# A four-layer graph kernel on one core: TensorE's passes written out, one addition moved to VectorE, and a new interleaving of two groups

## The chip, the cores and the metric

The kernel runs on one core of one Trainium2 chip. The metric is the time of one execution in microseconds, measured on the device; lower is better. The kernel before takes 2250.71 us (median of 3 runs, 2248.42 to 2252.54).

## The reference, cut to what matters

128 boards of 64 tokens with 256 features each go through four layers. Each layer adds its output to x:

```python
h = relu(layernorm(x)); x = x + att0(h, adj)    # layer 0: 8 heads of 32, biases, six fixed masks and two from adj
h = relu(layernorm(x)); x = x + att1(h, adj)    # layer 1: 4 heads of 64, all masked by adj
h = relu(layernorm(x)); x = x + graph(h, adj)   # layer 2
h = relu(layernorm(x)); x = x + att3(h, adj)    # layer 3: as layer 1

def graph(h, adj):                              # 4 heads
    Wh = h @ W[head].T + bW[head];  e = Wh @ attn[head]
    A = tanh(where(adj, e @ Wh.T, 0))
    hp = relu(A @ Wh)
    ha = concat(hp) @ A_w.T;  hf = h @ fc_w.T
    c = sigmoid(hf @ g1_w.T + ha @ g2_w.T + gbias)
    return hf * c + ha * (1 - c)
```

The kernel computes the last line with the update of x as x + ha + 0.5 * (hf - ha) * (1 + tanh(z / 2)), where z is the argument of the sigmoid. So ha itself is added to x once: this is the addition that the change moves.

## The kernel before, in words

Four boards (256 tokens) are a group; there are 32 groups. Two groups are in work at a time, one in each of two slots, and each slot has its own buffers and four of the eight PSUM banks. A pass takes one group through each slot, so there are 16 passes.

A group's work is a list of 109 steps (lines 287 to 304), the same for all engines: `bn`, `stats`, `norm` (the layer norm), `turn` 0 and 1 (transposes of the normalised x), `q`, `k`, `v`, `scores`, `mask`, `max`, `soft`, `pt` (transposes of the probabilities), `heads`, `pv`, `out` for an attention layer; `r`, `e` 0 to 3, `h`, `s2`, `a`, `ah`, `hp`, `ha`, `hf`, `hat` (transposes of ha), `g`, `sum` for the graph layer. Every engine walks through this list and issues only what is its own in a step. Engines wait for each other through semaphores, whose values are counted from the pass number (`Counts`, line 124).

Matrices are split in two parts of reduced width, high and low, and multiplied in three products. ScalarE copies the high part of a result out of PSUM, VectorE then computes the low part, and TensorE needs both for what follows.

The order in which an engine takes the steps of the two slots is written out per engine in `ORDER` (line 100): a lag, and for each of slot 0's 109 steps the number of slot 1's steps that follow it. Slot 1 is behind by the lag; so in the first half of a pass slot 0 goes through layers 0 and 1 while slot 1 does its graph layer and layer 3 of the group before, and in the second half the roles are changed. `passes` (line 306) writes out the first pass, without slot 1's older steps. The 15 others are one loop of each engine (`eng.Fori`, line 326) over a body that is written once; at its head the values for the waits are worked out in registers (`eng.snap`). The rest of slot 1's last group follows the loop. TensorE's last step in the body is slot 1's `r`, VectorE's is slot 1's `e` 0, ScalarE's is slot 0's last `pv`.

GpSimd (line 393) has three kinds of work: the power -0.5 for each layer norm in `stats` (line 410), between VectorE's variance (line 941) and VectorE's normalisation (line 949); the row terms in `r` (line 415), which TensorE's `s2` reads (line 650); and in `hat` the addition of ha to x (line 423), which VectorE's `sum` waits for (line 1093). x of the next group of a slot is loaded by SyncE (line 350) as soon as the last `out` of the group before has been added (line 1028), and stored from another buffer.

Of the kernel before, what the change touches and what calls it, by code (L numbers as in the profile page):

```python
# [25 lines left out]
ALU = mybir.AluOpType  # L26
# [36 lines left out]
def constants():  # L63
# [22 lines left out]
    for part in (0, LO):  # L86
# [11 lines left out]


ORDER = {  # L100
# [5 lines left out]
    "act": (57, (  # L106
# [4 lines left out]
    "dve": (48, (  # L111
# [4 lines left out]
    "pool": (46, (  # L116
# [4 lines left out]
}  # L121


# [16 lines left out]
def build(nc, x_in, adjq_in, adjt_in, mats_in, cols_in, rows_in, cst_in, out):  # L140
    GROUPS = x_in.shape[0] // TOK
    ITERS = GROUPS // SLOTS
# [6 lines left out]
    with ctx:  # L149
# [23 lines left out]
        X, XN, HT, MASKA, MASKO, ADJ8, ADJT8, SMALL = ([] for _ in range(8))  # L173
# [45 lines left out]
        WIDE, AT, F, RS, CT = ([] for _ in range(5))  # L219
# [83 lines left out]
                       ("g", L2, 0), ("g", L2, 1), ("sum", L2, 0)])  # L303
        STEPS = att_steps(0) + att_steps(1) + L2_STEPS + att_steps(2)

        def passes(eng, step, order):

            n = len(STEPS)  # L310
            lag, merge = order
            assert len(merge) == n and sum(merge) == n

            def turn(first, now, before):
                done = 0
                for k in range(n):
                    step(0, STEPS[k], now)
                    for done in range(done + 1, done + merge[k] + 1):
                        if done > lag:
                            step(1, STEPS[done - lag - 1], now)  # L320
                        elif not first:
                            step(1, STEPS[n - lag + done - 1], before)

            turn(True, Counts(0), None)
            if ITERS > 1:
                with eng.Fori(0, ITERS - 1) as i:
                    turn(False, Counts(i + 1, eng.snap), Counts(i, eng.snap))
            last = Counts(ITERS - 1)
            for k in range(n - lag, n):
                step(1, STEPS[k], last)  # L330
# [62 lines left out]
        @block.gpsimd  # L393
        def _(pool):
            nc.gpsimd.memset(RAWR[SQ:P, :], 0.0).then_inc(setup["padded"], 1)
            pool.wait_ge(setup["padded"], 1)
            nc.gpsimd.memset(UPAD[:, :, :], 0.0)
            nc.gpsimd.memset(BPAD[:, :, :], 0.0)
            for s in range(SLOTS):
                last = nc.gpsimd.memset(ADJT8[s][:, :, :, :], 0.0)  # L400
            last.then_inc(setup["zeroed"], 1)

            def step(s, what, v):
                k, a, i = what
                sm = S[s]
                if k == "stats":

                    n = norm_count(a, v)
                    pool.wait_ge(sm["ve"], n)
                    nc.gpsimd.tensor_tensor(RSTD[s], VE[s], HALF.broadcast_to([P, TT]), ALU.pow  # L410
                                            ).then_inc(sm["rstd"], 1)
                elif k == "r":

                    pool.wait_ge(sm["r_lo"], v.once)
                    nc.gpsimd.tensor_tensor(
                        R4[s][:, :].rearrange("p (b h q) -> p b h q", h=H2, q=SQ),
                        RS[s][:, 0:TOK].bitcast(F32).rearrange("p (b q) -> p b q", q=SQ).unsqueeze(2).broadcast_to([P, NB, H2, SQ]),
                        HEADS.unsqueeze(1).unsqueeze(3).broadcast_to([P, NB, H2, SQ]), ALU.mult
                        ).then_inc(sm["r4_ready"], 1)
                elif k == "hat" and i == 0:  # L420

                    pool.wait_ge(sm["ha_sb"], v.once)
                    nc.gpsimd.tensor_tensor(X[s][:, :], X[s][:, :], F[s][:, 0:512], ALU.add).then_inc(sm["x_ha"], 1)  # L423

            pool.wait_ge(setup["consts"], 1)

            pool.wait_ge(setup["vec_ps"], 2)
            for s in range(SLOTS):
                last = nc.gpsimd.memset(RS[s][:, 0:TOK].bitcast(F32), 0.0)
            last.then_inc(setup["terms_zero"], 1)  # L430
            passes(pool, step, ORDER["pool"])


        @block.tensor
        def _(pe):
# [289 lines left out]
                else:  # L725
                    att(s, k, a, i, v)

            passes(pe, step, ORDER["pe"])


        @block.scalar
# [134 lines left out]
        def _(dve):  # L866
# [164 lines left out]
            def l2(s, k, i, v):  # L1031
                sm, n = S[s], v.once
# [22 lines left out]
                elif k == "s2":  # L1055

                    if i == 0:
                        dve.wait_ge(sm["adjT_in"], v.dma2)
                    dve.wait_ge(sm["tanh"], v.two[i])
                    seen = ADJT8[s][:, i, :, :].unsqueeze(2).broadcast_to([P, 2, H2, SQ])  # L1060
                    view = tanh_buf(s, i).rearrange("p (e h q) -> p e h q", e=2, h=H2)
                    tt(view, view, seen, ALU.mult).then_inc(sm["at_f"], 1)  # L1062
                elif k == "a":
                    dve.wait_ge(sm["at_hi"], v.two[i])
                    lo_part(AT[s][:, 1, i, :], tanh_buf(s, i), AT[s][:, 0, i, :]).then_inc(sm["at_lo"], 1)

                    dve.wait_ge(sm["rs_hi"], v.two[i])
                    at = slice(i * 512, i * 512 + 512)
                    lo_part(RS[s][32:SQ, at], bank(s, i)[32:SQ, :], RS[s][32:SQ, at]).then_inc(sm["rs_lo"], 1)
                elif k == "ah":  # L1070
                    at = slice(i * 512, i * 512 + 512)
                    for c in range(DC):
                        dve.wait_ge(sm["ah_hi"], v.four[2 * i + c])
                        lo_part(WIDE[s][:, 1, c, at], bank(s, 2 * (1 - i) + c), WIDE[s][:, 0, c, at]
                                ).then_inc(sm["ah_lo"], 1)
                elif k == "hp":
                    dve.wait_ge(sm["ct_hi"], v.four[i])
                    hi, lo = ((CT[s][:, 0, :], CT[s][:, 1, :]) if i % 2 == 0 else (AT[s][:, 0, 0, :], AT[s][:, 1, 0, :]))
                    stt(lo, bank(s, HEAD_BANKS[i % 2]), 0.0, hi.bitcast(F32), ALU.max, ALU.subtract).then_inc(sm["ct_lo"], 1)
                elif k == "hat":  # L1080
                    dve.wait_ge(sm["hat_hi"], v.two[i])
                    at = slice(i * TOK, i * TOK + TOK)
                    lo_part(CT[s][:, 1, at], bank(s, HAT_BANKS[i])[:, 0:TOK], CT[s][:, 0, at]).then_inc(sm["hat_lo"], 1)
                elif k == "g":

                    dve.wait_ge(sm["gate_t"], v.two[i])
                    diff = F[s][:, 512 + i * D:512 + i * D + D]
                    tt(diff, bank(s, G_BANKS[i])[:, 0:D], F[s][:, i * D:i * D + D], ALU.subtract).then_inc(sm["diff"], 1)
                    dve.wait_ge(sm["diff"], v.two[i])
                    stt(diff, XN[s][:, i * D:i * D + D], 1.0, diff, ALU.add, ALU.mult).then_inc(sm["gated"], 1)  # L1090
                elif k == "sum":

                    dve.wait_ge(sm["x_ha"], n)
                    dve.wait_ge(sm["gated"], v.two[1])
                    stt(X[s][:, :], F[s][:, 512:1024], 0.5, X[s][:, :], ALU.mult, ALU.add).then_inc(sm["res2"], 1)
# [44 lines left out]
```

## Time and profile before

| | before |
|---|---|
| median of 3 runs | 2250.71 us (2248.42 to 2252.54) |
| the profiled execution | 2248.06 us |
| its span, first to last instruction | 2245.9 us |
| TensorE busy | 2011.9 us, 90% of the span |
| VectorE busy | 1445.6 us, 64% |
| ScalarE busy | 1151.8 us, 51% |
| GpSimd busy | 192.2 us, 9% |
| mean granted TensorE clock | 0.967 of full speed |
| bytes moved by DMA | 30.66 MB |

The page gives the busy time of each engine, the span in 40 slices, the chain of work that ended last, and groups of instructions. Busy shares are means over the whole span. What TensorE waits for, and where in a pass, is read from the table of waits and from the timeline. In the timeline a row is an instruction or a few of one kind: start, duration, engine, line, operation, what it writes and reads, how many, and in brackets the time that the engine stood idle before it and what ended that. PE is TensorE, PEld its weight loads, DVE VectorE, ACT ScalarE, POOL GpSimd, SP SyncE.

### The profile page before, as it was taken

What the parts mean: (1) busy time and instruction counts of PE and PEld (TensorE: products, weight loads), DVE (VectorE), ACT (ScalarE), POOL (GpSimd) and SP (SyncE); (2) the same over time, 40 slices, a digit from 0 to 9 for tenths busy, and PEclk for the clock granted to TensorE, in tenths of its full rate; (3) what the DMA queues carried; (4) which work ended last, traced back from release to release, by engine and by line L of the source; (5) the groups of instructions that cost most, each with busy time, mean ns of one, the idle gap of its engine ahead of it and who ended that gap; (6) DMA issues with size and microseconds to landing.
All of it is one profiled execution on the core that took longest, in us unless ns stands there. A gap on an engine that the chain in (4) does not pass through costs nothing.

```text
span 2245.9 us, 53566 instructions
## 1 busy us (share of the span) xinstructions
PE 2011.9 (90%) x21228; PEld 1818.6 (81%) x21228; DVE 1445.6 (64%) x3769; ACT 1151.8 (51%) x3862; POOL 192.2 (9%) x203
## 2 busy tenths in 40 slices
PE   6699989899898989989899998989989899998997
PEld 5588878788887888878788887888888788887885
DVE  4466667667666667667666666666757666666663
ACT  3355555455455555555455454545455455455552
POOL 0000101100001100100110000100101100000100
PEclk8799999999999999999999999999999999999998
DMA  5000000000000000000000000000000000000000
GB/s 174 1 3 12 12 12 12 11 5 9 12 12 12 11 11 2 11 12 11 12 11 2 12 11 12 11 11 2 11 12 11 11 12 2 12 11 12 11 6 5
DMA packets 40630, 30.66 MB, mean 14 GB/s; under 512 B 15664, under 2 KB 40240, under 8 KB 40432
## 3 DMA queue, kind: packets, MB, share of 16 engines
q1 hardware_dynamic: 40432, 27.48, 4.1%
q8 instruction: 190, 3.11, 0.6%
q14 instruction: 8, 0.07, 0.0%
HBM read 19.08 MB, written 8.39 MB: 12 GB/s over the span
## 4 chain that ended last, share of the span: by engine, by line
PE 62%; issue 18%; DVE 12%; ACT 4%; POOL 4%; DMA 1%; DVEq 0%; SPq 0%; POOLq 0%; ACTq 0%
PE ps L437 57%; PE ps L505 4%; POOL small L410 3%; DVE small L931 2%; DVE xn L949 2%; PE ps L581 2%; ACT probs L788 1%; DVE x L1028 1%; DVE wide L1053 1%; DVE f L1062 1%; POOL x L423 1%; DVE aT L870 1%; ACT f L824 1%; ACT wide L816 1%; DVE small L938 1%
## 5 line engine op out<-in xcount | busy, mean ns | idle before, releaser
L437 PE MATMUL ps<-hT,w_hi 128*128 128x256 f32 x2560 | 511.2, 291 | 55.8 <-issue 47.7
L437 PEld LDWEIGHTS ps<-hT,w_hi 128*128 128x128 f32 x2560 | 420.5, 194 | 73.1 <-issue 50.8
L788 ACT ACTIVATE probs<-probs,small 128x64 f32<-128x64 f32 x1024 | 342.1, 339 | 33.2 <-DVE small L1009 31.4
L437 PE MATMUL ps<-hT,w_lo 128*128 128x256 f32 x1280 | 343.1, 288 | 0.0
L437 PEld LDWEIGHTS ps<-hT,w_lo 128*128 128x128 f32 x1280 | 249.2, 195 | 2.7
L437 PE MATMUL ps<-w_hi,hT 128*128 128x256 f32 (+1 forms) x1024 | 249.1, 312 | 0.0
L410 POOL TENSOR_TENSOR small<-small,consts 128x2 f32<-128x2 f32 x128 | 88.8, 694 | 1776.2 <-DVE small L941 1776.2
L437 PE MATMUL ps<-w_hi,oT 128*128 128x256 f32 x768 | 189.2, 311 | 27.4 <-DVE oT L870 27.4
L437 PE MATMUL ps<-wide,w_hi 128*128 128x256 f32 x1024 | 213.1, 285 | 0.2
L788 ACT ACTIVATION_READ_ACCUMULATOR probs<-probs,small 128x1 f32 x1024 | 196.2, 192 | 0.0
L816 ACT ACTIVATE wide<-ps,c_vec 128x256 fp32r<-128x256 f32 x256 | 107.6, 472 | 148.3 <-PE ps L437 148.3
L437 PEld LDWEIGHTS ps<-w_hi,hT 128*128 128x128 f32 x1024 | 175.4, 188 | 8.4
L1053 DVE SCALAR_TENSOR_TENSOR wide<-ps,c_vec,wide 128x256 fp32r<-128x256 f32 x256 | 109.5, 479 | 103.6 <-ACT wide L816 103.5
L437 PEld LDWEIGHTS ps<-w_hi,oT 128*128 128x128 f32 x768 | 147.5, 211 | 32.5 <-DVE oT L870 32.3
L437 PEld LDWEIGHTS ps<-wide,w_hi 128*128 128x128 f32 x1024 | 163.4, 188 | 3.1 <-DVE wide L870 0.7
L949 DVE TENSOR_SCALAR xn<-x,small 128x256 f32<-128x256 f32 x256 | 123.3, 523 | 62.0 <-POOL small L410 59.7
L437 PE MATMUL ps<-w_hi,cT 128*128 128x256 f32 x768 | 159.3, 290 | 0.3 <-ACT cT L848 0.3
L505 PE MATMUL ps<-consts,xn 128*128 128x128 f32 x512 | 116.3, 324 | 46.1 <-DVE xn L949 42.9
L437 PE MATMUL ps<-w_lo,hT 128*128 128x256 f32 (+1 forms) x512 | 149.9, 310 | 0.0
L763 ACT ACTIVATE hT<-ps 128x256 fp32r<-128x256 f32 x256 | 88.4, 383 | 98.5 <-PE ps L505 97.6
L505 PEld LDWEIGHTS ps<-consts,xn 128*128 128x128 f32 x512 | 62.5, 151 | 86.9 <-DVE xn L949 74.2
L437 PE MATMUL ps<-wide,w_lo 128*128 128x256 f32 x512 | 131.8, 280 | 0.0
(123 smaller groups left out, 4342.5 us busy)
## 6 DMA issues: line engine op xcount, KB each, us to landing
raw_mats<-mats SPq DMA_DIRECT2D x8, 1024.0 KB, 11.9
x<-x SPq DMA_DIRECT2D x32, 256.0 KB, 3.0
out<-xn SPq DMA_DIRECT2D x32, 256.0 KB, 3.0
adj<-adjq SPq DMA_DIRECT2D x64, 16.0 KB, 2.0
adjT<-adjt SPq DMA_DIRECT2D x64, 8.0 KB, 2.1
raw_consts<-board_consts SPq DMA_DIRECT2D x1, 451.5 KB, 3.1
raw_rows<-rows SPq DMA_DIRECT2D x1, 256.0 KB, 4.5
bias_cols<-cols SPq DMA_DIRECT2D x1, 6.0 KB, 3.6
```

Source lines behind the costliest of these rows:

```text
L410: nc.gpsimd.tensor_tensor(RSTD[s], VE[s], HALF.broadcast_to([P, TT]), ALU.pow).then_inc(sm["rstd"], 1)
L423: nc.gpsimd.tensor_tensor(X[s][:, :], X[s][:, :], F[s][:, 0:512], ALU.add).then_inc(sm["x_ha"], 1)
L437: return nc.tensor.matmul(o, lhsT, rhs, start=start, stop=stop, skip_group_check=True)
L505: last = nc.tensor.transpose(bank(s, H_BANKS[c])[:, t * P:t * P + P], XN[s][:, t * D + c * P:t * D + c * P + P], IDENT)
L581: last = nc.tensor.transpose(bank(s, 1 - i)[:, at:at + P], PR[s][:, j, at:at + P], IDENT)
L763: fn(HT[s][:, 0, c, :], bank(s, H_BANKS[c])[:, 0:TOK], ACT.Relu).then_inc(S[s]["hT_hi"], 1)
L788: last = fn(p, p, ACT.Exp, bias=ROWMAX[s][:, row:row + 1], accum_out=ROWSUM[s][:, row:row + 1])
L816: last = fn(e_view(s, 0, oc, i), e_bank(s, E_BANKS[i], oc), ACT.Identity, bias=CVEC[:, oc, i:i + 1])
L824: fn(tanh_buf(s, i), bank(s, 2 + i), ACT.Tanh).then_inc(sm["tanh"], 1)
L931: nc.vector.bn_stats(STATS[s][:, t, :], X[s][:, t * D:t * D + D]).then_inc(S[s]["bn"], 1)
L949: ts(XN[s][:, t * D:t * D + D], X[s][:, t * D:t * D + D], MV[s][:, t, 0:1], RSTD[s][:, t:t + 1], ALU.subtract, ALU.mult).then_inc(S[s]["xn ...
L1053: stt(e_view(s, 1, oc, i), e_bank(s, E_BANKS[i], oc), CVEC[:, oc, i:i + 1], e_view(s, 0, oc, i).bitcast(F32), ALU.add, ALU.subtract).then_ ...
```

## The change

Three things are changed.

1. TensorE's passes are written out one behind the other, with constants in place of registers in the waits. The other engines keep their loops.
2. The addition of ha to x is taken from GpSimd's step `hat` and put into VectorE's step `hat` 0, ahead of VectorE's low parts there. It has the same wait (`ha_sb`, set by ScalarE's copy of ha at line 844) and raises the same semaphore.
3. The lags and merge lists of all four engines are replaced. TensorE's lag goes from 49 to 48, ScalarE's from 57 to 46, VectorE's stays at 48, GpSimd's goes from 46 to 37.

```diff
 ORDER = {
-    "pe": (49, (
+    "pe": (48, (
...
-    "act": (57, (
+    "act": (46, (
...
     "dve": (48, (
...
-    "pool": (46, (
+    "pool": (37, (
...
-        def passes(eng, step, order):
+        def passes(eng, step, order, unrolled=False):
...
             turn(True, Counts(0), None)
-            if ITERS > 1:
+            if unrolled:
+                for i in range(1, ITERS):
+                    turn(False, Counts(i), Counts(i - 1))
+            elif ITERS > 1:
                 with eng.Fori(0, ITERS - 1) as i:
                     turn(False, Counts(i + 1, eng.snap), Counts(i, eng.snap))
...
-                elif k == "hat" and i == 0:
-
-                    pool.wait_ge(sm["ha_sb"], v.once)
-                    nc.gpsimd.tensor_tensor(X[s][:, :], X[s][:, :], F[s][:, 0:512], ALU.add).then_inc(sm["x_ha"], 1)
...
-            passes(pe, step, ORDER["pe"])
+            passes(pe, step, ORDER["pe"], unrolled=True)
...
                 elif k == "hat":
+                    if i == 0:
+
+                        dve.wait_ge(sm["ha_sb"], n)
+                        tt(X[s][:, :], X[s][:, :], F[s][:, 0:512], ALU.add).then_inc(sm["x_ha"], 1)
                     dve.wait_ge(sm["hat_hi"], v.two[i])
```

The merge lists, written as sequences (0: and 1: are the slots; layers are 0, 1, graph, 3), differ in these places:

```
TensorE, end of slot 1's layer 3:  before  1:heads, 0:turn 0 1, 1:out 0 1, 0:r          after  1:heads, 1:out 0, 0:turn 0 1, 1:out 1, 0:r
TensorE, slot 1's graph layer:     before  1:ha 1, 0:pt 0, 1:hp 3, 0:pt 1, 1:hf 0       after  1:ha 1, 1:hp 3, 0:pt 0, 0:pt 1, 1:hf 0
TensorE, last of the body:         before  1:r                                          after  1:r, 1:e 0
VectorE, end of slot 1's layer 3:  before  1:soft, 0:out 0 1, 0:bn 0, 1:soft, 0:bn 1, 0:stats, 0:norm, 1:pv 0 1, 0:turn 0, 1:out 0, 0:turn 1, 1:out 1
                                   after   0:out 0, 1:soft, 1:soft, 0:out 1, 0:bn 0 1, 0:stats, 1:pv 0 1, 0:norm, 1:out 0, 0:turn 0 1, 1:out 1
VectorE, start of a group:         before  e 3, h, masks, (s2 0), turn 0, turn 1        after  e 3, masks, turn 0, h, turn 1, s2 0
ScalarE, start of slot 0's group:  before  1:e 3, 1:h, 1:s2 0, 0:turn 0 1, 1:s2 1       after  1:e 3, 0:turn 0, 1:h, 0:turn 1, 1:s2 0 1
ScalarE, last of the body:         before  0:pv 1 of layer 3                            after  1:e 2
GpSimd, slot 0's graph layer:      before  0:stats, 0:r, 1:stats of layer 0             after  0:stats, 1:stats of layer 0, 0:r
```

In the last row the power of slot 1's next group stands ahead of the row terms of slot 0.

## Rows read from the trace of the kernel before

**Rows 1.** The page: span, and each engine's busy time, share, instructions.
```profile
span 2245.9 us, 53566 instructions
...
PE 2011.9 (90%) x21228; PEld 1818.6 (81%) x21228; DVE 1445.6 (64%) x3769; ACT 1151.8 (51%) x3862; POOL 192.2 (9%) x203
```

**Rows 2.** PE's waits, whole run: total us, times, longest us.
```profile
PE ps L437 <- issue: 50.0, 18, 3.8
...
PE ps L505 <- DVE xn L949: 42.9, 59, 4.9
```

**Rows 3.** Stretches with the jump: length, busy time (instructions), PE's clock, DMA share.
```profile
408.63:477.60 68.97, 61.52 (x660) 55.59 (x659) 44.29 (x117) 35.48 (x120) 5.92 (x7) 0.98 0.04 10
...
sum 973.08, PE 868.62 PEld 786.73 DVE 620.86 ACT 497.08 POOL 82.96; mean PE 62.04 PEld 56.20 DVE 44.35 ACT 35.51 POOL 5.93
```

**Rows 4.** The same of the 13 stretches without it.
```profile
342.91:408.63 65.72, 61.47 (x660) 55.79 (x659) 44.63 (x117) 35.28 (x120) 5.93 (x8) 0.97 0.04 10
477.60:541.94 64.34, 60.07 (x660) 54.38 (x659) 44.63 (x117) 35.17 (x120) 5.93 (x7) 1.00 0.04 10
...
sum 843.34, PE 787.85 PEld 713.95 DVE 580.38 ACT 457.83 POOL 77.09; mean PE 60.60 PEld 54.92 DVE 44.64 ACT 35.22 POOL 5.93
```

**Rows 5.** Timeline of PE at the jump: last of "r", first of "e".
```profile
1912.77 0.86 PE L437 MATMUL ps<-hT,u_vec 128*36 128x256 f32 x6
...
1916.90 0.36 PE L437 MATMUL ps<-hT,w_hi 128*128 128x256 f32 x1 [3.27 <-issue]
```

**Rows 6.** Timelines of ACT and DVE at the same jump.
```profile
1918.61 0.84 ACT L816 ACTIVATE wide<-ps,c_vec 128x256 fp32r<-128x256 f32 x2 [4.47 <-PE ps L437]
...
1919.48 0.88 DVE L1053 SCALAR_TENSOR_TENSOR wide<-ps,c_vec,wide 128x256 fp32r<-128x256 f32 x2 [4.83 <-ACT wide L816]
1920.27 0.74 DVE L931 BATCH_NORM_STATS2 small<-x 128x6 f32<-128x256 f32 x2
```

**Rows 7.** Timeline of PE where the first pass enters the loop.
```profile
168.79 0.86 PE L437 MATMUL ps<-hT,u_vec 128*36 128x256 f32 x6
169.49 0.36 PE L437 MATMUL ps<-hT,w_hi 128*128 128x256 f32 x1
```

**Rows 8.** DMA queue of instructions, 1886.82 to 1955.62 (jump), then 1955.62 to 2019.97: packets, MB.
```profile
q8 instruction: 7, 0.11, 0.7%
...
q8 instruction: 5, 0.08, 0.5%
```

**Rows 9.** Timelines of POOL, DVE and PE around the addition of ha.
```profile
2019.97 1.28 POOL L423 TENSOR_TENSOR x<-x,f 128x512 f32<-128x512 f32 x1
...
2020.05 1.68 DVE L949 TENSOR_SCALAR xn<-x,small 128x256 f32<-128x256 f32 x2 [0.81 <-POOL small L410]
...
2025.28 0.69 DVE L1095 SCALAR_TENSOR_TENSOR x<-f,x 128x512 f32<-128x512 f32 x1
...
2027.27 0.68 DVE L989 COPY kT<-ps 128x512 f32<-128x512 f32 x1
2028.18 0.73 DVE L949 TENSOR_SCALAR xn<-x,small 128x256 f32<-128x256 f32 x2 [0.23 <-POOL small L410]
...
2021.46 0.87 PE L505 MATMUL ps<-consts,xn 128*128 128x128 f32 x4 [0.55 <-DVE xn L949]
...
2028.06 0.69 PE L437 MATMUL ps<-kT,qT 64*64 64x64 f32 x32
```

**Rows 10.** Timelines of SP, POOL and PE at slot 0's "s2"; the page's landing of x.
```profile
1981.57 0.38 SPq L350 DMA_DIRECT2D x<-x  x1
...
1982.64 1.92 POOL L415 TENSOR_TENSOR row_terms<-rs,consts 128x1024 fp32r<-128x1024 f32 x1 [4.89 <-DVE rs L1048]
1986.10 0.69 POOL L410 TENSOR_TENSOR small<-small,consts 128x2 f32<-128x2 f32 x1 [1.55 <-DVE small L941]
...
1989.71 0.39 PE L437 MATMUL ps<-row_terms,sel_rows 128*128 128x512 f32 x1
...
x<-x SPq DMA_DIRECT2D x32, 256.0 KB, 3.0
```

32 rows, old and new, of the table ORDER are left out of this document.

## The prediction

> **What bounds the kernel now.** I read the page first: TensorE (PE) is busy 90% of the span, VectorE 64%, ScalarE 51%, GpSimd 9% [rows 1]. So the end is set by PE and by what it waits for. The table of PE's waits comes next [rows 2]: the largest single entry is "issue", 50.0 us in 18 pieces, time in which PE waited for no engine; behind it come waits for VectorE's normalised x. To see where these fall I cut the steady part into halves of a pass, from one GpSimd addition of the graph layer's output (line 423) to the next; the addition is made once for each of the 32 groups of four boards. Between 272.48 and 2088.90 us they alternate: 14 halves hold the jump from the end of PE's loop body (slot 1's step "r") back to its start, 13 do not. PE does the same 660 matmuls in each, but the 14 sum to 973.08 us, 69.51 each [rows 3], and the 13 to 843.34 us, 64.87 each [rows 4]. Those 13 are of two kinds: eight of 64.3 to 64.4 us at full granted clock, five of 65.6 to 65.8 with the clock at 0.97 [rows 4].
>
> The jump itself: after the six small matmuls of "r" PE stands still for 3.27 us with nothing to wait for [rows 5]; the 14 pieces in the other passes are 3.2 to 3.8 us. ScalarE and VectorE then wait 4.47 and 4.83 us, all of it PE's lateness [rows 6]. Is it the jump, or the register arithmetic at the head of the body that works out the values of the waits? The first pass is written out and falls into the loop body through that same head without a jump: there "e" follows "r" at once, 0.70 us after its start, with no gap [rows 7]. So it is the jump. What it does is seen in the instruction queue's DMA: 7 blocks of 16 KB in a half with the jump, 5 in one without [rows 8].
>
> **Part 1: PE's passes written out.** Removed: 14 jumps (15 looped passes; the entry and the exit cost none). What follows at a place without a jump is shown by the straight halves, which do the same work, so I use them as the price: 973.08 - 14 x 64.87 = 64.9 us. The gaps themselves are at most 50.0 of them [rows 2]; the rest is that TensorE is at the lower of its clocks, 1.2 instead of 2.4 GHz, for a few us more in such halves (PE busy is 62.04 us in them against 60.60) [rows 3, 4]. I take the mean of the straight halves and not the fastest (64.34), since short waits remain that let the clock fall in some halves: that is the choice in this term. With no fall at all the saving would be 973.08 + 843.34 - 27 x 64.34 = 79.2 us; with a fall in every half (65.72 [rows 4]) it would be 973.08 + 843.34 - 27 x 65.72 = 42.0 us. Added: nothing on PE but a longer stream. 5 blocks per 64.3 us were fetched in straight halves without any gap, so I price streaming at 0.
>
> The Trainium skill, "Runtime: NRT & Kernel Launch", section "Instruction fetch mechanics", says that an engine prefetches instructions only in sequence, 16 KiB at a time, that PE holds 2048 of them and the other engines 512, and that a jump outside this window waits for a fetch. The trace agrees for PE, which runs about 2,650 instructions a pass (21228 matmuls and as many weight loads over 16 passes [rows 1]) and fetches two blocks more when it jumps. By the rule ScalarE (3862 / 16 = 241 instructions a pass) and VectorE (3769 / 16 = 236 [rows 1]) need no fetch at their own jumps, which stay; were it otherwise, rival 2 below would be the forecast.
>
> **Part 2: the addition moves from GpSimd to VectorE.** Before: GpSimd adds for 1.28 us at 2019.97; VectorE's two normalisations (line 949), which start 0.08 us later, take 1.68 us, against 0.73 for the same pair where GpSimd is quiet, and PE waits 0.55 us for them before its transposes [rows 9]. After: that pair costs 0.73, so 0.95 less on VectorE; the addition there costs one 128x512 operation, for which I take the 0.69 us of the similar line 1095 [rows 9]. VectorE's chain behind it is thus 0.26 us earlier. PE's transposes could start 0.55 us earlier, but four steps on PE's "scores" start at 2028.06 while VectorE's copy of k, which they need, ends at 2027.95 [rows 9]: only 0.11 us of slack, so PE keeps 0.25, not 0.55. 32 groups x 0.25 = 8.0 us gained. Bounds: a gain of 0.55 x 32 = 17.6; or, if the slow pair were not GpSimd's doing, VectorE is 0.69 later, of which two idle moments of about 0.17 each before its next operations absorb half: a loss of 0.35 x 32 = 11 us. I take 8.0, nearest to the row of the quiet pair.
>
> On this the Trainium skill, "SBUF — State Buffer", section "SBUF: two separate sides", says that VectorE and GpSimd share one pair of ports, held by one of them for a whole instruction. By that the 0.95 us return in full (the gain of 8.0); by a reading in which the norms are slow for another reason the loss of 11 stands. The trace sides with the rule, 1.68 against 0.73.
>
> **Part 3: the turns laid out anew.** From the merge lists: on PE, in the halves where slot 1 ends its last attention layer, "out" 0 of slot 1 goes ahead of slot 0's graph-layer transposes, where before it followed them; "hp" 3 moves ahead of "pt" 0 there; the jump's place moves by one "e". The wait before those transposes was 0.46 us for VectorE's x; now PE waits about as long for VectorE's low part of the heads' output instead. VectorE does "pv" (0.75) while GpSimd's power runs (0.8 us in which it was idle), but its layer sum comes one 0.42 us operation later. I price this at 0, bounds -0.46 and +0.46 us in each of 16 halves: -7 to +7 us. On ScalarE and VectorE the second transposed half is taken before the first tanh or masking, and masked scores ahead of a remainder; each swaps neighbours of 0.4 to 0.7 us whose readers are later steps: 0, within the same bounds. ScalarE's and VectorE's jumps stay, and GpSimd's; old waits of 4.47 and 4.83 us lay over them [rows 6], VectorE's first operation behind its jump (bn) began as the one before it ended. No row shows these jumps uncovered; bounds 0 and, from that cover, 4.8 us each time; I take 0 because their entries into the loop and their instruction fetches show nothing [rows 7, 8].
>
> GpSimd: slot 1's first power now stands ahead of slot 0's row terms (line 415). Before, these ran 1982.64 to 1984.56 and the power at 1986.10; now they queue behind the power: 1986.79 + 1.92 = 1988.71. PE reads them at 1989.71 [rows 10]. Slack 1.0 us: cost 0, but this cover is thin, and the power waits for x from HBM, issued at 1981.57 and landing in 3.0 us [rows 10].
>
> **Sum.** Against the profiled execution, 2248.06 us (span 2245.9 [rows 1] and 2.2 around it): 2248.06 - 64.9 - 8.0 + 0 = 2175.2 us. The median before is 2250.71, 2.65 more; the same offset gives 2177.8. I say 2177.
>
> **Rivals.**
> 1. *TensorE's clock falls in every half.* The waits of 0.5 to 1.1 us around "pt" and "heads" stay and nothing anchors them to the jump. For: all 14 halves with the jump show less than full clock, and five straight ones do. Against: eight straight halves run at 1.00 [rows 4]. Time: 2248.06 - 42.0 - 8.0 = 2198, on the median's scale 2201.
> 2. *The other engines' jumps come to light.* They sit at the same place (VectorE's behind slot 1's "e" 0, ScalarE's now between "e" 2 and "e" 3, with "s2" waiting for all four), and so far a wait of 4.5 us lay over them. For: there was always cover, so nothing excludes it. Against: rows 7 and 8 as above. If they cost 3.27 us like PE's: 14 x 3.27 = 46 back, 2178 + 46 = 2224.
> 3. *Slower than before: row terms behind x.* The chain x from HBM, bn, power, row terms, "s2" has 1.0 us of slack. If slot 1's x lands late, slot 0's "s2" stands with it, on PE, in 16 halves. To eat the 73 us gained it must be 1.0 + 73/16 = 5.6 us late each time, a landing of 8.6 us instead of 3.0; at 10 us it is 16 x 6.0 = 96 lost, 2274. Against: the median landing is 3.0 us [rows 10], and the DMA engines are busy 4% of a half [rows 4].
> 4. *The change does not do what it says:* the written-out stream stalls at block borders as it did at the jump. 5 blocks a half without a gap [rows 8] speak against; one 3.27 us stall a half would leave no gain (2250).
>
> **Chances.** Forecast with its own spread (2152 to 2192: the saving of part 1 up to 79, parts 2 and 3 by their bounds) 0.68; rival 1 0.18; rival 2, in whole or part, 0.08; rival 3 0.03; rival 4 0.03. The low end is 2248.06 - 79.2 - 17.6 = 2151, plus the offset 2154; I go to 2153. The high end takes in rival 1 and a little of rival 2: 2206. A measurement of this kernel tells 0.2% (4.5 us) from nothing: faster 0.94, within 0.03, slower 0.03.
>
> **What would show it.** Right: PE's "issue" waits fall from 50 to a few us; the gap between "r" and "e" is gone in every pass; all halves are alike, near 64.6 us (64.87 - 0.25); the pair at line 949 beside the addition takes 0.73; the wait of 0.55 before the transposes is gone; instruction blocks fall by two a pass. Wrong: granted clock below 1.00 in each half (rival 1); VectorE or ScalarE idle between its "e" steps once a pass with PE waiting at "s2" (rival 2); PE waiting for row terms (rival 3); an addition that costs VectorE more than 0.69.

## The result: 2.7% faster, at the slow end of the forecast

| | median | ratio to before, 95% interval |
|---|---|---|
| before | 2251.62 us (4 runs) | |
| changed | 2193.66 us (4 runs, 2188.86 to 2197.49) | 0.9734 [0.9697, 0.9771] |
| changed again, in another series | 2188.44 us (before there: 2262.61) | 0.9672 [0.9649, 0.9694] |

The forecast was 2177 (2153 to 2206). The sign, the range and the leading cause hold; 17 us are missing on that scale, 13.7 in the profiled execution (2188.86 against 2175.2).

The medians of the kernel before differ between series (2251.6, 2266.5, 2262.6, 2256.8, 2254.4), so ratios are taken within a series.

The page after, span and engines, answers to [rows 1]; then the page's instruction queue, which before had 190 packets:

```profile
span 2186.7 us, 52980 instructions
PE 1994.9 (91%) x21228; PEld 1808.3 (83%) x21228; DVE 1464.7 (67%) x3801; ACT 1150.5 (53%) x3862; POOL 151.3 (7%) x171
...
q8 instruction: 167, 2.74, 0.5%
```

PE's waits after, as [rows 2] (in the changed kernel most lines are one less than before: 504 is the transposes of x, 948 the normalisation, 436 the products):

```profile
PE ps L580 <- DVE probs L1018: 48.1, 54, 3.3
PE ps L504 <- DVE xn L948: 42.1, 21, 4.9
PE ps L436 <- DVE oT L869: 38.8, 49, 0.9
PE ps L436 <- issue: 18.4, 36, 0.7
```

"Issue" has fallen from 50.0 us to 18.4 and no piece is over 0.7. Most of what is left are pieces of 0.52 us ahead of "heads", at a place where the kernel before waited 0.56 us for ScalarE's copy; the gap of the jump is gone. But the wait for VectorE's normalised x is as large as before, 42.1 against 42.9, and in 21 pieces instead of 59: something new waits there.

The halves, from one addition of ha to the next as in [rows 3, 4]. The first two rows are a neighbouring pair at full clock, the third one in which the clock fell, the last the sum of 28 halves:

```profile
533.06:596.77 63.71, 60.13 (x660) 54.62 (x659) 44.23 (x119) 35.09 (x120) 4.67 (x5) 1.00 0.04 10
596.77:661.91 65.14, 60.07 (x660) 54.51 (x659) 45.72 (x120) 35.39 (x120) 4.63 (x5) 1.00 0.04 10
...
466.48:533.06 66.58, 61.53 (x660) 55.95 (x659) 45.93 (x120) 35.52 (x120) 4.63 (x5) 0.97 0.04 10
...
sum 1821.72, PE 1698.67 PEld 1544.13 DVE 1261.71 ACT 988.52 POOL 130.24; mean PE 60.67 PEld 55.15 DVE 45.06 ACT 35.30 POOL 4.65
```

28 halves take 65.06 us each on the mean; 64.62 was forecast. The half that had the jump went from 68.8 to 63.7. The half that had none went from 64.34 [rows 4] to 65.14, although PE's busy time in it is the same (60.07): it has got slower by 0.8, and its VectorE is busy 1.1 us longer (45.72 against 44.63).

**Where that is.** Timelines of POOL, DVE and PE of the changed kernel at slot 0's "e" steps in such a half; the last DVE row is the same place 64 us earlier, in the good half:

```profile
625.81 0.69 POOL L413 TENSOR_TENSOR small<-small,consts 128x2 f32<-128x2 f32 x1 [7.69 <-DVE small L940]
626.47 1.91 POOL L418 TENSOR_TENSOR row_terms<-rs,consts 128x1024 fp32r<-128x1024 f32 x1
...
624.39 0.74 DVE L930 BATCH_NORM_STATS2 small<-x 128x6 f32<-128x256 f32 x2
...
626.62 2.23 DVE L948 TENSOR_SCALAR xn<-x,small 128x256 f32<-128x256 f32 x2
...
628.58 0.87 PE L504 MATMUL ps<-consts,xn 128*128 128x128 f32 x4 [1.56 <-DVE xn L948]
...
562.91 0.73 DVE L948 TENSOR_SCALAR xn<-x,small 128x256 f32<-128x256 f32 x2
```

GpSimd's row terms now start 0.15 us ahead of the two normalisations, and these take 2.23 us instead of 0.73: they end at 628.85, 0.47 us after the row terms (628.38). In [rows 9] the pair also ends 0.48 us after GpSimd's addition. PE waits 1.56 us. It is the case of [rows 9] once more, with the row terms in the addition's part. x itself was there in time: bn (line 930) starts as VectorE's step before it ends.

At the old place, the addition moved as forecast. DVE and PE of the changed kernel there:

```profile
596.12 0.73 DVE L948 TENSOR_SCALAR xn<-x,small 128x256 f32<-128x256 f32 x2 [0.80 <-POOL small L413]
596.77 0.68 DVE L1083 TENSOR_TENSOR x<-x,f 128x512 f32<-128x512 f32 x1
...
602.91 0.69 DVE L988 COPY kT<-ps 128x512 f32<-128x512 f32 x1
...
596.82 0.63 PE L504 MATMUL ps<-consts,xn 128*128 128x128 f32 x4
603.70 0.70 PE L436 MATMUL ps<-kT,qT 64*64 64x64 f32 x32
```

The pair is at 0.73, the addition costs 0.68, PE does not wait for its transposes. From the start of the pair to "scores" it is 7.58 us, against 8.01 in [rows 9].

### The profile page after: what moved, and what is told of

Its sections match the earlier page's. It is cut to its first block, busy times and chain, and to the rows that moved or that the text cites. A ratio compares the mean times of both kernels' runs of the same rounds, so it can differ in the third digit from the quotient of the medians.

```text
span 2186.7 us, 52980 instructions
## 1 busy us (share of the span) xinstructions
PE 1994.9 (91%) x21228; PEld 1808.3 (83%) x21228; DVE 1464.7 (67%) x3801; ACT 1150.5 (53%) x3862; POOL 151.3 (7%) x171
## 4 chain that ended last, share of the span: by engine, by line
PE 71%; DVE 11%; issue 9%; ACT 7%; DMA 1%; POOL 1%; DVEq 0%; SPq 0%; POOLq 0%; ACTq 0%
PE ps L436 65%; ACT probs L787 3%; PE ps L504 3%; PE ps L580 2%; DVE wide L1052 2%; DVE small L930 2%; ACT oT L797 1%; DVE probs L1018 1%; DVE aT L869 1%; DVE xn L948 1%; POOL small L413 1%; ACT wide L815 1%; DVE x L1027 1%; ACT hT L762 1%; PE ps L713 1%
## 5 line engine op out<-in xcount | busy, mean ns | idle before, releaser
L436 PE MATMUL ps<-hT,w_hi 128*128 128x256 f32 x2560 | 499.9, 287 | 8.1 <-ACT hT L762 7.9
L436 PEld LDWEIGHTS ps<-hT,w_hi 128*128 128x128 f32 x2560 | 412.5, 191 | 21.2 <-ACT hT L762 16.7
L436 PE MATMUL ps<-hT,w_lo 128*128 128x256 f32 x1280 | 338.0, 284 | 0.0
L436 PE MATMUL ps<-w_hi,cT 128*128 128x256 f32 x768 | 170.2, 300 | 0.3 <-ACT cT L847 0.3
L948 DVE TENSOR_SCALAR xn<-x,small 128x256 f32<-128x256 f32 x256 | 117.9, 502 | 49.8 <-POOL small L413 47.1
L504 PE MATMUL ps<-consts,xn 128*128 128x128 f32 x512 | 103.5, 309 | 43.9 <-DVE xn L948 42.1
L436 PEld LDWEIGHTS ps<-w_hi,cT 128*128 128x128 f32 x768 | 126.2, 188 | 9.6 <-ACT cT L847 0.5
```

The lines of the kernel that those rows point to most:

```text
L436: return nc.tensor.matmul(o, lhsT, rhs, start=start, stop=stop, skip_group_check=True)
L504: last = nc.tensor.transpose(bank(s, H_BANKS[c])[:, t * P:t * P + P], XN[s][:, t * D + c * P:t * D + c * P + P], IDENT)
L948: ts(XN[s][:, t * D:t * D + D], X[s][:, t * D:t * D + D], MV[s][:, t, 0:1], RSTD[s][:, t:t + 1], ALU.subtract, ALU.mult).then_inc(S[s]["xn ...
```

## The experiments

My theory after this result: writing out gives what was forecast; GpSimd's new order costs 1.5 us in every second half; TensorE's clock takes part of whatever is gained. The rivals: late x, the other engines' jumps, and new orders that are good or bad in themselves. The twelve runs were timed beside the kernel before in four series: e1, e2, e3 and f1; g1, a1, h1 and f2; i1, i2 and i3; h2.

**e1, writing out alone.** The kernel before with only this:

```diff
-            passes(pe, step, ORDER["pe"])
+            passes(pe, step, ORDER["pe"], unrolled=True)
```

> The kernel before with TensorE's passes written out and nothing else (old orders, addition on GpSimd). Theory: the 14 jumps go and every half costs what a straight half costs, 64.87 us on the mean: 65 us less than before, about 2187 (2179 to 2196); VectorE's first operation behind its own jump starts when the one before it ends, and PE shows no wait between r and e. Rival (the jumps of VectorE, ScalarE and GpSimd come to light once TensorE's no longer covers them): the halves with the jumps stay above 66 us although PE has none, 2205 or more, with PE waiting at s2 or at turn once a pass.

Measured: 2184.86 us against 2266.46, ratio 0.9645 [0.9617, 0.9673]. The halves:

```profile
402.52:467.02 64.50, 60.28 (x660) 54.49 (x659) 44.29 (x117) 35.30 (x120) 5.93 (x7) 1.00 0.03 10
467.02:532.25 65.23, 61.24 (x660) 55.66 (x659) 44.63 (x117) 35.40 (x120) 5.93 (x7) 0.97 0.04 10
...
sum 1816.53, PE 1698.61 PEld 1538.48 DVE 1245.96 ACT 989.67 POOL 166.12; mean PE 60.66 PEld 54.95 DVE 44.50 ACT 35.35 POOL 5.93
```

64.88 us a half, where my price was 64.87. That it meets to a hundredth is luck: six executions of e1 differ by 7.5 us, 0.2 us a half, and the clock fell in 12 of its 28 halves against 5 of the 13 straight ones. Its profiled execution is 65 us below the one that the forecast started from; in its own series the saving is 82 us and not 65, since the kernel before stood at 2266 there. No half shows the other engines' jumps. And writing out alone is as fast as the whole change.

**e2, the addition alone.** The kernel before with line 423 moved into VectorE's "hat" 0, as in the change.

> The kernel before with the addition of ha to x on VectorE instead of GpSimd and nothing else. Theory: the pair of normalisations beside it falls from 1.68 to 0.73 us, the addition costs VectorE 0.69, PE's wait of 0.55 before the transposes goes, and 0.25 us a group stay: 8 us less than before, 2243 (2236 to 2248). Rival (VectorE's chain gains nothing, its longer work is paid elsewhere): 2251 to 2262.

Measured: 2273.60 us against 2266.46, ratio 1.0017 [0.9995, 1.0038]. No gain. The 8 us that I expected did not come. Yet at full clock its straight halves are 63.83 to 63.89, 0.5 less than [rows 4]. The clock took it: 0.93 in most halves with the jump and 0.97 in most without. Over whole executions the mean granted clock was 0.942 to 0.948 in all twelve of e2, and 0.953 to 0.961 in the kernel before of the same series.

```profile
618.98:682.87 63.89, 60.17 (x659) 54.48 (x658) 44.22 (x119) 35.03 (x120) 4.68 (x5) 1.00 0.04 10
1225.50:1296.63 71.13, 63.89 (x661) 58.45 (x659) 44.10 (x119) 35.38 (x121) 4.68 (x5) 0.93 0.04 10
```

**e3, the orders alone.** The kernel before with the four new `ORDER` entries.

> The kernel before with the four new orders and nothing else (TensorE keeps its loop, the addition stays on GpSimd). Theory: the new place of GpSimd's row terms, behind the power of slot 1's next group, puts them beside VectorE's two normalisations of that group; these take 2.2 us instead of 0.73 and PE waits 1.5 us before their transposes, in each of 16 passes: 24 us, partly given back by the other moves (0.3 us in the other halves): 2251 + 20 = 2271 (2262 to 2278). Rival (the new orders are neutral or good by themselves, and the wait comes from x being loaded late once TensorE runs faster): 2240 to 2253, since the loop's gap leaves the load its old room.

Measured: 2241.37 us against 2266.46, ratio 0.9888 [0.9857, 0.9919]. That is 25 us less than before: the theory said 20 more, and the rival at most 11 less. (2241 lies within the rival's range only because the kernel before took 2266 in this series.) The wait of 1.57 us for x is there, in a kernel whose loop still has its jump: so late x after a faster TensorE is not its cause. But the halves with the jump are 66.0, not 68.8, because the jump's gap has shrunk. PE there:

```profile
1905.16 0.86 PE L437 MATMUL ps<-hT,u_vec 128*36 128x256 f32 x6
...
1908.79 0.36 PE L437 MATMUL ps<-hT,w_hi 128*128 128x256 f32 x1 [1.35 <-issue]
```

"e" 0 now stands ahead of the jump. Its 12 matmuls (24 instructions with their weight loads, 1.44 us; g1's expectation calls them 24 matmuls) run before the gap, and the gap is 1.35 us and not 3.27. That PE's sequencer is already jumping while they run is my reading; it leaves 0.5 of the 1.9 us unexplained.

**g1, the changed kernel with TensorE's loop put back**, that is without the line of e1.

> The changed kernel with TensorE's loop put back (new orders, addition on VectorE). Theory: under the new orders the jump stands behind slot 1's e 0, whose 24 matmuls PE's sequencer has already handed on when it jumps, so it costs about 2 us and not 3.3, 14 times, and the halves without a jump keep their 65.2: about 2222 (2212 to 2232), so writing out is worth 28 to 35 us here and not 65. Rival (the jump costs what it cost before, 4.5 us a pass): 2250 or more.

Measured: 2219.13 us against 2262.61, ratio 0.9809 [0.9782, 0.9836]; the changed kernel again, as a1, 2188.44 in the same series.

> The changed kernel as it is, once more beside the others of this call. 2194 (2188 to 2198), as before; what is compared with it in this call is free of the chip and the hour.

As expected: with the new orders writing out is worth 31 us, with the old ones 82 (e1). The orders had already taken part of the jump away, so the two gains don't add.

**f1, row terms first.** The changed kernel with GpSimd's old order:

```diff
-    "pool": (37, (
+    "pool": (46, (
```

> The changed kernel with GpSimd's old order: the row terms of slot 0 run before the power of slot 1's next group, as they did before the change. Theory: the row terms leave the port before the normalisations start, these fall from 2.2 to 0.73 us, PE's wait of 1.56 us before the transposes goes, and all halves are near 63.7 us: 16 x 1.5 = 24 less than 2194, 2170 (2163 to 2180). Rival (x lands late): nothing changes, 2190 to 2197. Second rival (TensorE's clock falls more often when the halves are shorter and all alike): half of it is given back, 2182.

Measured: 2182.64 us against 2266.46, ratio 0.9630 [0.9600, 0.9659]. That the late normalisations come from GpSimd's order is shown. The timeline of f1's DVE at the pair:

```profile
1145.78 0.74 DVE L948 TENSOR_SCALAR xn<-x,small 128x256 f32<-128x256 f32 x2
```

The windows of f1's halves, two at full clock, one not, and the sum of 28:

```profile
1052.13:1115.89 63.76, 60.23 (x660) 54.67 (x659) 44.30 (x119) 35.17 (x120) 4.67 (x5) 1.00 0.04 11
1115.89:1179.63 63.74, 60.05 (x660) 54.64 (x659) 44.23 (x119) 35.21 (x120) 4.67 (x5) 1.00 0.03 10
...
466.64:531.72 65.08, 61.41 (x660) 55.98 (x659) 44.40 (x120) 35.33 (x120) 4.67 (x5) 0.97 0.04 10
...
sum 1816.79, PE 1715.17 PEld 1563.50 DVE 1242.38 ACT 987.45 POOL 130.84; mean PE 61.26 PEld 55.84 DVE 44.37 ACT 35.27 POOL 4.67
```

The pair is at 0.74 and both halves are at 63.75 where the clock is full. But it is full in 6 of 28 halves only, against 17 of 28 in the changed kernel. The mean is 64.89 again. This is the second rival of the expectation, and the time is its 2182.

What TensorE did before a fall, in the half that begins at 466.64: it waited 0.85, 0.23, 0.55, 0.52 and 0.72 us between 481.7 and 488.1, around "out", "pt" and "heads", and right behind that the granted clock is at its lower level:

```profile
486.64 0.69 PE L436 MATMUL ps<-probsT,v 64*64 64x64 f32 x32 [0.52 <-issue]
488.05 0.58 PE L436 MATMUL ps<-w_hi,oT 128*128 128x256 f32 x1 [0.72 <-DVE oT L869]
...
488.64:490.64 2.00, 2.00 (x11) 2.00 (x11) 0.76 (x3) 0.26 (x1) 0.00 (x0) 0.50 0.00 0
```

But the half at 1115.89, at full clock throughout, has the same five waits to 0.01 us. So the waits alone do not decide whether the clock falls.

**h1, the waits filled.** f1 with 12 extra matmuls a group, of 256 columns and 0.12 us each, which write into a free bank and which nobody reads:

```diff
+                    if a == 2 and i == 1:      # ahead of "pt" 1
+                        keep_busy(s, 5)
...
+                    if a == 2:                 # ahead of "heads"
+                        keep_busy(s, 2)
...
+                        if a == 1:             # ahead of "out" 0
+                            keep_busy(1 - s, 5)
```

> The changed kernel with GpSimd's row terms first (as f1) and extra matmuls whose result nobody reads, into a bank that is free, where TensorE waits for the softmax chain: 5 before out 0 of layer 1, 5 before pt 1 and 2 before heads of layer 3, 0.12 us each, in every group. Theory (in f1 what the lock gave back was lost to TensorE's clock, which falls after these short waits): with the waits filled the clock stays at 1.00 and all halves are near 63.8 us: 2183 - 25 x 1.3 = 2150 (2143 to 2165). Rival (the clock falls for another reason, or the halves are bound by the other engines): the extra matmuls change nothing or cost up to 12 x 0.12 x 32 = 46 us: 2180 to 2229.

Measured: 2150.06 us (2149.57 to 2152.79) against 2262.61, ratio 0.9504 [0.9485, 0.9524]. Every one of the 28 halves is at full clock:

```profile
719.01:782.81 63.80, 61.66 (x672) 56.23 (x671) 44.20 (x119) 35.19 (x120) 4.68 (x5) 1.00 0.04 11
782.81:846.54 63.73, 61.80 (x672) 56.21 (x671) 44.26 (x120) 35.15 (x120) 4.67 (x5) 1.00 0.04 10
...
sum 1786.80, PE 1728.44 PEld 1573.44 DVE 1238.63 ACT 984.84 POOL 130.86; mean PE 61.73 PEld 56.19 DVE 44.24 ACT 35.17 POOL 4.67
```

More work for TensorE and some 32 us less (f2, below, is as fast as f1 and took 2181.93 us in this series): this version beats both kernels.

**h2, the same extra matmuls elsewhere**: all 12 inside "e" 1, where f1's PE does not wait.

> As f1, with the same 12 extra matmuls a group as h1, whose result nobody reads, but all of them inside the run of e steps, where TensorE never waits. Theory (it is the filling of the waits that holds the clock): the clock falls as in f1, 0.97 in most halves, and the 12 x 0.12 = 1.44 us a half are added: 2183 + 31 x 1.44 = 2227 (2205 to 2232). Rival (any extra work for TensorE holds the clock): full clock in all halves, 2150 + 45 = 2195 (2190 to 2200).

Measured: 2206.12 us against 2254.35, ratio 0.9787 [0.9761, 0.9813]. The time lies between what the two theories give, at the low edge of the first one's range, and neither is right about the clock. In h1 the 12 matmuls lie in time in which PE waited; here they add to its path, 65.16 - 63.75 = 1.4 us a half at full clock, so the time is not to be set beside f1's as it stands. (They also bring a new wait of 0.58 us for ScalarE ahead of "s2"; the other waits are as in f1.) What tells is the clock: it falls in 8 of 28 halves, fewer than in f1 (22), more than in h1 (none):

```profile
538.39:603.55 65.16, 61.16 (x672) 56.02 (x671) 44.29 (x119) 35.06 (x120) 4.67 (x5) 1.00 0.04 10
799.15:865.82 66.67, 62.67 (x672) 57.49 (x671) 44.30 (x119) 35.05 (x120) 4.67 (x5) 0.97 0.03 10
```

So filling f1's waits removes the falls, but extra work elsewhere removes many of them too, and how often the clock falls after an unfilled wait depends on more than the wait. On what, no run here tells.

**f2, all engines written out**: f1 with `unrolled=True` for the other three as well.

> As f1 (changed kernel, row terms first), with the passes of VectorE, ScalarE and GpSimd written out too. Theory: their jumps cost nothing that PE sees: 2183, as f1 (2179 to 2187). Rival (each of them costs a fraction of a microsecond a pass on the path): 5 to 20 us less, 2163 to 2178.

Measured: 2181.93 us against 2262.61, ratio 0.9650 [0.9628, 0.9671], where f1 has 0.9630 [0.9600, 0.9659]. The jumps of the other engines cost nothing that the total shows. At full clock four of f2's halves are 63.61 to 63.72 and f1's 63.73 to 63.79, so the jumps may cost up to 0.1 us a half, which these totals cannot tell from nothing.

**i1, i2, i3: what the parts are worth when the clock does not fall.** All have the 12 extra matmuls of h1. i1 is e1 with them, i2 the changed kernel with them, i3 is h1 with the addition back on GpSimd.

> As e1 (the kernel before, only TensorE's passes written out) with the 12 extra matmuls a group of h1, whose result nobody reads. It shows what writing out is worth by itself when the clock does not fall. Theory: all halves at the 64.5 us that e1 shows where its clock is full, so 2150 + 30 x 0.75 = 2172 (2165 to 2180), 12 under e1. Rival (the old orders' halves shrink to h1's 63.8 once the clock holds, so the addition and the orders are worth nothing): 2150.

> The changed kernel, with GpSimd's order as the change has it, and the 12 extra matmuls a group of h1. It shows the price of the row terms' new place when the clock does not fall. Theory: every second half waits 1.4 to 1.6 us for VectorE's x: 2150 + 15 x 1.45 = 2172 (2167 to 2177). Rival (the wait for x costs no more than the 5 to 9 us by which f1 and the changed kernel differ): 2155 to 2160.

> As h1 with the addition of ha to x back on GpSimd. It shows what the addition's place is worth when the clock does not fall. Theory: the pair of normalisations beside it is at 1.68 us again and PE waits 0.55 us for it, of which 0.25 to 0.5 stays in each of 32 groups: 2150 + 8 to 16 = 2158 to 2166. Rival (nothing stays, the chain of VectorE absorbs it): 2150.

Measured in one series, before 2256.82: i1 2180.28, ratio 0.9655 [0.9626, 0.9683]; i2 2178.51, 0.9646 [0.9620, 0.9672]; i3 2170.33, 0.9618 [0.9593, 0.9644]. A typical half at full clock of i1:

```profile
595.98:660.47 64.49, 61.73 (x672) 55.95 (x671) 44.62 (x117) 35.17 (x120) 5.91 (x7) 1.00 0.04 10
```

A pair of i2, whose first half is the one with the late row terms:

```profile
1379.48:1444.69 65.21, 61.73 (x672) 56.08 (x671) 45.73 (x119) 35.43 (x120) 4.63 (x5) 1.00 0.04 10
1444.69:1508.41 63.72, 61.74 (x672) 56.17 (x671) 44.24 (x120) 35.10 (x120) 4.67 (x5) 1.00 0.04 11
```

And a pair of i3, which is at full clock in all 28 halves:

```profile
984.08:1048.27 64.19, 61.64 (x672) 56.04 (x671) 44.65 (x117) 35.36 (x120) 5.93 (x7) 1.00 0.04 10
1048.27:1112.62 64.35, 61.86 (x672) 56.07 (x671) 44.66 (x117) 35.25 (x120) 5.94 (x8) 1.00 0.03 10
```

With h1's 63.75 beside them, a half at full clock is: old orders 64.48; new orders but row terms first 64.27, so 0.2 gained; addition on VectorE besides 63.75, so 0.52 gained; row terms as in the change (65.20 + 63.72) / 2 = 64.46, so 0.71 lost. Times 32 groups that is 16.6 us gained by the addition and 22.7 lost by the place of the row terms.

The medians say the same with some error, since h1 ran in another series: i3 to h1 20 us gained, h1 to i2 28 lost, i1 to i3 10 gained. i2's clock fell in 2 of 28 halves, i1's in 6; i1 missed its expectation by 8 us and i2 by 6. A likely reason, not tested, is that the extra matmuls had been counted out for f1's order and cover i1's waits less well. And in i1 the filling gained nothing: its ratio is 0.9655, e1's without it 0.9645. In i2 it gained little: 0.9646, against 0.9672 and 0.9734 of the changed kernel. Only on f1's order is it worth 32 us. Taken together, the addition and the orders of the change are worth nothing beside writing out: i1 and i2 differ by 2 us.

## Why the prediction was right, and where it was not

**Part 1, writing out: right.** "What follows at a place without a jump is shown by the straight halves": 64.87 was the price, e1 measures 64.88. The choice of the mean and not of the fastest was the right one; the fastest, 64.34, would have given 14 us too much. "Issue" falls to pieces of 0.7 at most, and blocks fall by 23 (two a pass would be 28). That the register arithmetic is free and the jump alone costs still rests on [rows 7]: e1 takes out both. A slip without effect: the prediction speaks of a gap of 3.27 us and 14 in the other passes; there are 14 in all. The saving is no fixed price, though: in their series 82 us beside the old orders, 31 beside the new ones.

**Part 2, the addition: right in kind, half in size.** The pair fell to 0.73 and the addition costs 0.68. I took 0.25 a group and gave 0.55 as the bound; it is 0.52 at full clock (i3 against h1). The term that was off is the chain of VectorE from the pair to the copy of k: 7.90 us in [rows 9] and 7.48 after, so 0.42 earlier and not 0.26. By the starts of VectorE's operations the pair and the addition give 0.34 of it, since the next operation starts 0.60 us after the addition and not 0.69; the two low parts behind them take 0.22 less, as a wait for ScalarE is gone; and 0.14 is lost again further on. Only lengths of operations were in my sum. On like orders, i3 against h1, the same stretch is 7.91 and 7.41 us (two halves of each), 0.50 less, and PE's scores start 0.10 us behind the copy in all of them: that is the 0.52.

**Part 3, the orders: the step that failed.** "Slack 1.0 us: cost 0", for row terms that queue behind the power and that PE reads 1.0 us after they end. From the start of the power to the end of the row terms it is 2.57 us, and 2.61 was worked out. The reader was looked at, and the neighbour was not: behind that same power VectorE normalises x. Part 2 had just priced such a meeting from [rows 9] (0.95 us). With row terms of 1.91 us it costs 2.23 - 0.73 = 1.5 us. In 16 halves that is 24 us against the 0 of my sum (22.7 by the halves of i2 and h1), and well outside the 7 that part 3 gave as the bounds of its other moves. It took back the addition's gain. The Trainium skill, "SBUF — State Buffer", section "SBUF: two separate sides", which I cited in part 2, says that whichever of the two engines comes first holds the shared ports for its whole instruction. The trace agrees: both times GpSimd was first, and both times VectorE's pair ended 0.47 to 0.48 us after GpSimd's instruction.

**The clock (rival 1): half right.** I held it for one case in five that the clock falls in every half. In the changed kernel it falls in 11 of 28 halves, in f1 in 22, in h1 in none. In f1's order it costs more than any term of parts 2 and 3: 32 us from f2 to h1.

**Rival 2 fell** with e1 and f2. **Rival 3** had its place right (power, row terms, "s2") and its cause wrong: PE waits for x normalised late, not for the row terms, and x from HBM is in time. **Rival 4** fell: 167 blocks, no stall.

In sum, in the profiled execution: forecast 2175.2; row terms +24, addition 0.27 x 32 more = -9, orders' own 0.2 x 32 = -6; that makes 2184 against 2188.86. The remaining 5 us are not accounted for; the clock may be in them, but no run splits them off. That the total came within 14 us is in part luck: a cost of 24 us and gains of 15 us, all beyond the sum, partly cancel.

## What to carry to other kernels

Before an instruction of GpSimd or VectorE is moved, look at what the other of the two does beside it at the new place, and not only at who waits for its result. Price a jump by the stretch without it, and see what is queued ahead of the jump: with 1.44 us of work there the gap was 1.35 us and not 3.27. When a gain on the path does not arrive in the total, read the granted clock of each stretch: here a half in which it fell mostly took 1.1 to 1.5 us longer in f1 (64.8 to 65.3 against 63.75), and a half with waits of the same length did not lose it. Filling the waits with work that nobody needs gained 32 us on one order of steps and nothing on another (e1 to i1), so it has to be measured on each.

## What the runs showed of the hardware that I had not expected

Kernels of different length at full clock have nearly one mean half: the straight halves before 64.87, e1 64.88, f1 64.89, f2 64.85 us, though their halves without a fall are 64.34, 64.50, 63.75 and mostly 63.6 to 63.7. The clock fell in 5 of 13, 12, 22 and 23 of 28. The changed kernel does not quite fit: 65.06 us, and 65.15 in a1. Whether it is one effect or chance is not settled; no run here tells it.

The kernel before varied from 2242 to 2279 us between runs, h1 by 3.2 us in five. A clock that never falls is not needed for a steady time, though: f1, with 22 falls in its profile, varied by 2.7 us in five, and e3, with 16, by 1.4.
